# A transformer layer with a mixture of experts: the last two expert tiles without VectorE, plain second gathers, and the final normalising shared between two engines

## The reference, cut to what matters

```python
logits = x_flat @ w_router
top_vals, top_idx = jax.lax.top_k(logits, 2)
probs = jax.nn.softmax(top_vals, axis=-1)
h = jnp.einsum('nc,ecd->ned', x_flat, w_fc)        # 8 experts, 512 x 512
h = jnp.square(jax.nn.relu(h))
y = jnp.einsum('ned,edc->nec', h, w_proj)
out = jnp.einsum('nec,ne->nc', y, w_tok)           # weights of the two chosen experts
x = _layernorm(x + out, axis=-1)
```

## Time and profile before

| | |
|---|---|
| Median of 3 runs | 1472.44 us |
| The profiled execution | 1470.72 us |
| Its span, first to last instruction | 1469.0 us |
| TensorE busy | 1428.9 us (97%) |
| VectorE busy | 771.4 us (53%) |
| ScalarE busy | 727.3 us (50%) |
| GpSimd busy | 415.4 us (28%) |
| Granted TensorE clock, mean | 0.995 of full speed |

### The profile page before, as it was taken

One profiled execution on the slowest core, in us unless ns is written; L12 is line 12 of the kernel. 1 busy time (PEld: TensorE's weight loads), 2 busy tenths in 40 slices (PEclk: granted clock), 3 DMA queues, 4 the chain that ended last, 5 costly groups with the idle time before them and its releaser, 6 DMA issues. The chain is left out here.

```text
span 1469.0 us, 26596 instructions
## 1 busy us (share of the span) xinstructions
PE 1428.9 (97%) x7998; PEld 1209.6 (82%) x7999; DVE 771.4 (53%) x1813; ACT 727.3 (50%) x1633; POOL 415.4 (28%) x410
## 2 busy tenths in 40 slices
PE   8999999999999999999999999989999989999994
PEld 6888888888888888888888888878888867888883
DVE  6555655655555655555555565545555563333334
ACT  5665655655656565556565565622222223333334
POOL 1212121212112212122121121103333445345575
PEclk9999999999999999999999999999999999999997
DMA  5243323232323333233323235433348446665699
GB/s 176 77 129 93 107 93 127 86 114 85 115 93 107 111 111 100 100 98 102 108 93 128 93 107 179 144 123 125 136 121 224 123 172 215 253 247 200 211 199 235
DMA packets 86547, 200.45 MB, mean 136 GB/s; under 512 B 15856, under 2 KB 16496, under 8 KB 83184
## 3 DMA queue, kind: packets, MB, share of 16 engines
q1 hardware_dynamic: 75728, 149.66, 31.2%
q0 software_dynamic: 10784, 50.36, 12.0%
HBM read 160.05 MB, written 92.62 MB: 172 GB/s over the span
## 5 line engine op out<-in xcount | busy, mean ns | idle before, releaser
L378 POOL TENSOR_TENSOR small<-small,half 128x4 f32<-128x4 f32 x193 | 194.9, 1010 | 768.8 <-DVE small L408 768.8
L511 DVE CUSTOM_DVE_ANT_0 logit<-score_ps,bias 128x128 f32<-128x128 f32 (+3 forms) x256 | 124.8, 487 | 157.0 <-PE score_ps L650 117.6
L312 ACT ACTIVATE prob<-logit,small 128x128 f32<-128x128 f32 (+3 forms) x256 | 144.2, 563 | 120.5 <-DVE small L511 116.8
L663 PEld LDWEIGHTS y_ps<-vs,prob_t 128*128 128x128 f32 x1280 | 175.0, 191 | 20.4 <-issue 3.7
L663 PE MATMUL y_ps<-vs,prob_t 128*128 (+1 forms) x1280 | 184.7, 275 | 0.3 <-DVE x_now L412 0.3
L319 ACT ACTIVATE prob_t<-prob_ps 128x128 f32<-128x128 f32 (+3 forms) x256 | 111.6, 436 | 54.4 <-PE prob_ps L656 53.4
L894 ACT ACTIVATE yt_hi<-turn_ps,subln 128x512 fp32r<-128x512 f32 x60 | 41.0, 688 | 154.1 <-PE turn_ps L1188 150.2
L656 PE MATMUL prob_ps<-ident,prob 128*128 128x128 f32 x640 | 112.7, 274 | 3.2 <-ACT prob L312 3.0
L576 PE MATMUL v_ps<-w_hi,x_hi 128*128 (+1 forms) x256 | 106.8, 417 | 1.3 <-DVE w_lo L447 1.3
L576 PE MATMUL v_ps<-w_hi,x_lo 128*128 (+1 forms) x256 | 106.3, 415 | 0.0
L576 PE MATMUL k_ps<-w_hi,x_hi 128*128 (+1 forms) x256 | 103.2, 403 | 0.6 <-DVE w_lo L447 0.6
(11 more groups left out here) (250 smaller groups left out, 3421.5 us busy)
## 6 DMA issues: line engine op xcount, KB each, us to landing
slots_x<-in_zeros SPq DMA_DIRECT2D x64, 512.0 KB, 5.2
y_scratch<-x_now SPq DMA_DIRECT2D x65, 256.0 KB, 2.9
x_raw<-in_x_t SPq DMA_DIRECT2D x64, 256.0 KB, 2.8
slots_y<-in_zeros SPq DMA_DIRECT2D x64, 256.0 KB, 5.1
y_raw<-y_scratch SPq DMA_DIRECT2D x14, 1024.0 KB
w_raw<-in_w_experts POOLq DMA_DIRECT2D x7, 2048.0 KB
w_hi<-in_w_experts POOLq DMA_DIRECT2D x7, 2048.0 KB
w_raw<-in_w_all SPq DMA_DIRECT2D x16, 768.0 KB, 6.5
```

The source lines that it names most:

```text
L312: nc.scalar.activation(prob[:, 0:width], logit[:, 0:width], ACT.Exp, scale=-1.0, bias=least[:, h:h + 1], accum_out=row_sum[:, (i % 2) * HG ...
L378: nc.gpsimd.tensor_tensor(r, ms, half[:, :], ALU.pow).then_inc(ready, 1)
L511: nc.vector.tensor_tensor_reduce(out=logit[:, 0:width], in0=score_ps[:, 0:width], in1=bias[:, h, T - width:T], scale=1.0, scalar=3e38, op0 ...
L663: mm = nc.tensor.matmul(y_ps[:, h * D:(h + 1) * D], prob_t[:, j * P:(j + 1) * P], one(vs[:, bass.ds(now, 1), j, h * D:(h + 1) * D]), start ...
```

## The change

In slot steps 37 and 38 (`ALONE` and after) VectorE and SP have no part. ScalarE squares (from `relu`, with the Square function) and copies the low part; TensorE computes that low part: it multiplies the tile by the identity into the accumulator that already held the turned tile and then adds minus the identity times the high part (`turn_remainder`), between the sixth and seventh matmul of the next product, or at once in step 38. ScalarE issues the stores of the two slot tiles. (With 39 slot tiles, the branch for the rows of tile k + 2 is never taken in steps 37 and 38.)

The second gathers of tiles 8 to 15 go without addition to `w_raw`; VectorE adds them to `x1`. The aggregate of a tile stands right behind its statistics. Batches are 4, 4, 4 and 4 tiles. The root of the first batch is issued on GpSimd behind second gather 7, that of the second behind gather 11, the last two behind gather 15. VectorE normalises twelve tiles: 0 to 3 behind the statistics of tile 5, 4 to 7 behind those of 9, 8 and 9 behind those of 14, and 12 and 13 at the end; ScalarE normalises 10, 11, 14 and 15.

```diff
+        negative = sb("negative", [P, P], F32R)
-        END_BATCHES = ((0, 4), (4, 8), (8, 12), (12, 14), (14, 16))
+        END_BATCHES = ((0, 4), (4, 8), (8, 12), (12, 16))
+        PLAIN = range(8, 16)
+        ACT_TILES = (10, 11, 14, 15)
+        ALONE = SLOT_TILES - 2
...
@@ slots_sync @@
             def slot_step(k, b, h, y, q):
+                if alone(k):
+                    return
...
             for t in range(NT):
-                sp.wait_ge(fin_ready, t + 1)
+                done = sum(u in ACT_TILES for u in range(t + 1))
+                if t in ACT_TILES:
+                    sp.wait_ge(fin_scaled, done)
+                else:
+                    sp.wait_ge(fin_ready, t + 1 - done)
                 sp.dma_start(out_tiles[t], x1[:, t, :]).then_inc(fin_stored, 16)
...
@@ slots_gpsimd @@
-                gather(t, 1, second_gathered[t % GB])
-            pool.wait_ge(end_set_up, 1)
-            for first, last in END_BATCHES:
-                end_inverse_std(first, last)
+                if t in PLAIN:
+                    pool.indirect_dma_start(w_raw[:, t % GB, :], None, slots_y,
+                                            bass.IndirectOffsetOnAxis(ap=slot_y[:, 1, t:t + 1], axis=0))\
+                        .then_inc(second_gathered[t % GB], 16)
+                else:
+                    gather(t, 1, second_gathered[t % GB])
+                if t == GB - 1:
+                    pool.wait_ge(end_set_up, 1)
+                    end_inverse_std(*END_BATCHES[0])
+                if t == GB + RB - 1:
+                    end_inverse_std(*END_BATCHES[1])
+            end_inverse_std(*END_BATCHES[2])
+            end_inverse_std(*END_BATCHES[3])
...
@@ slots_scalar @@
+            nc.scalar.activation(negative[:, :], ident[:, :], ACT.Copy, scale=-1.0).then_inc(negative_set, 1)
...
             def slot_step(k, b, h, y, q):
                 round_hid(b, k)
+                if alone(k):
+                    act.wait_ge(hid_rest, k - ALONE + 1)
+                    nc.scalar.activation(ht_lo[:, b, :], ht_ps[b][:, :], ACT.Copy).then_inc(ht_ready, 1)
                 if more(k, 1):
                     rectify(1 - b, k + 1)
+                    if alone(k):
+                        act.wait_ge(relu_done, k + 2)
+                        nc.scalar.activation(hid[:, 1 - b, :], relu[:, :], ACT.Square).then_inc(hid_ready, 1)
...
                 scale_out(k, b, y, q)
+                if alone(k):
+                    act.wait_ge(yo_ready, k + 1)
+                    act.nop(nofuse=True)
+                    nc.scalar.dma_start(y_slot[k], yo[:, y, :]).then_inc(yo_stored[y], 16)
...
-            for t in range(NT):
-                act.wait_ge(mean_ready, t + 1)
+            for n, t in enumerate(ACT_TILES):
+                act.wait_ge(mean_ready, n // 2 + 1)
                 nc.scalar.activation(x1[:, t, :], x1[:, t, :], ACT.Identity, scale=end_rstd[:, t:t + 1],
-                                     bias=minus_mean[:, t:t + 1]).then_inc(fin_ready, 1)
+                                     bias=minus_mean[:, t:t + 1]).then_inc(fin_scaled, 1)
...
@@ slots_vector @@
             def slot_step(k, b, h, y, q):
+                if alone(k):
+                    return
...
+            def normalise_rows(first, last):
                 dve.wait_ge(end_rstd_ready, last)
-                nc.vector.scalar_tensor_tensor(minus_mean[:, first:last], end_mean_var[:, first:last, 0], -1.0,
-                                               end_rstd[:, first:last], ALU.mult, ALU.mult)\
-                    .then_inc(mean_ready, last - first)
+                if first >= GB:
+                    nc.vector.scalar_tensor_tensor(minus_mean[:, first + 2:last], end_mean_var[:, first + 2:last, 0], -1.0,
+                                                   end_rstd[:, first + 2:last], ALU.mult, ALU.mult).then_inc(mean_ready, 1)
+                    last = first + 2
+                for t in range(first, last):
+                    nc.vector.tensor_scalar(x1[:, t, :], x1[:, t, :], end_mean_var[:, t, 0:1], end_rstd[:, t:t + 1],
+                                            ALU.subtract, ALU.mult).then_inc(fin_ready, 1)
...
             for t in range(NT):
                 dve.wait_ge(second_gathered[t % GB], 16 * (t // GB + 1))
+                if t in PLAIN:
+                    if t == PLAIN[0]:
+                        dve.wait_ge(first_gathered[t // GB], 16 * GB)
+                    nc.vector.tensor_tensor(x1[:, t, :], x1[:, t, :], w_raw[:, t % GB, :], ALU.add)\
+                        .then_inc(rows_summed, 1)
+                    dve.wait_ge(rows_summed, t - PLAIN[0] + 1)
                 nc.vector.bn_stats(end_stats[:, t, :], x1[:, t, :]).then_inc(end_stats_done, 1)
-                if t >= 1:
-                    aggregate(t - 1)
+                aggregate(t)
+                if t % RB == RB - 1:
+                    bias_variance(t + 1 - RB, t + 1)
+                if t == RB + 1:
+                    normalise_rows(*END_BATCHES[0])
+                if t == GB + 1:
+                    normalise_rows(*END_BATCHES[1])
+                if t == NT - 2:
+                    normalise_rows(*END_BATCHES[2])
+            normalise_rows(*END_BATCHES[3])
...
@@ slots_tensor @@
+            def turn_remainder(out, src, hi, b, rounded, count, done):
+                pe.wait_ge(rounded, count)
+                for c in range(CT):
+                    nc.tensor.matmul(out[:, c * P:(c + 1) * P], src[:, b, c * P:(c + 1) * P], ident[:, :],
+                                     start=(c == 0), stop=False)
+                nc.tensor.matmul(out[:, :], negative[:, :], hi[:, b, :], start=False, stop=True).then_inc(done, 1)
```

More of the change, by code:

```diff
@@ L1312, in more, with alone @@
             return (k if isinstance(k, int) else YB * LOOPED - 1) + ahead < SLOT_TILES
+        def alone(k):
+            return isinstance(k, int) and k >= ALONE
         def slots_sync(sp):
@@ L1366, in slots_sync @@
             for t in range(NT):
-                sp.wait_ge(fin_ready, t + 1)
+                done = sum(u in ACT_TILES for u in range(t + 1))
[3 more added lines that the diff above has]
+                    sp.wait_ge(fin_ready, t + 1 - done)
                 sp.dma_start(out_tiles[t], x1[:, t, :]).then_inc(fin_stored, 16)
             sp.wait_ge(fin_stored, 16 * NT)
+            for y in range(YB):
+                sp.wait_ge(yo_stored[y], 16 * ((SLOT_TILES - 1 - y) // YB + 2))
         def slots_gpsimd(pool, token_step, inverse_std, dispatch, send_gates):
@@ L1619, in slots_vector @@
             for t in range(NT):
                 dve.wait_ge(second_gathered[t % GB], 16 * (t // GB + 1))
-                nc.vector.bn_stats(end_stats[:, t, :], x1[:, t, :]).then_inc(end_stats_done, 1)
-                if t >= 1:
-                    aggregate(t - 1)
[L1624 to L1629, removed]
@@ L1639, in turn_x, with times @@
                 mm.then_inc(xs_turned, 1)
-            def times(out, b, hi, lo, first_block, first=0, last=3 * CT):
+            def turn_remainder(out, src, hi, b, rounded, count, done):
[4 more added lines that the diff above has]
+                nc.tensor.matmul(out[:, :], negative[:, :], hi[:, b, :], start=False, stop=True).then_inc(done, 1)
+            def times(out, b, hi, lo, first_block, first=0, last=3 * CT, between=None):
                 for s in range(first, last):
                     c, part = divmod(s, 3)
+                    if s == 6 and between is not None:
+                        between()
                     a = (hi, hi, lo)[part][:, b, c * P:(c + 1) * P]
@@ L1652, in load_owner, with up @@
                 return pe.value_load(at, min_val=0, max_val=E - 1)
-            def up(b, e, count):
+            def up(b, e, count, between=None):
                 pe.wait_ge(xt_ready, count)
                 pe.wait_ge(we_split, WT * e + WT)
-                times(h_ps[b], b, xt_hi, xt_lo, expert_block(e)).then_inc(up_done, 1)
+                times(h_ps[b], b, xt_hi, xt_lo, expert_block(e), between=between).then_inc(up_done, 1)
             def turn_hid(b, k):
@@ L1663, in turn_hid, with down @@
                 mm.then_inc(hid_turned, 1)
-            def down(b, e, k):
+            def down(b, e, k, between=None):
                 pe.wait_ge(ht_ready, k + 1)
-                times(ye_ps[b], b, ht_hi, ht_lo, expert_block(e) + CT).then_inc(down_done, 1)
+                times(ye_ps[b], b, ht_hi, ht_lo, expert_block(e) + CT, between=between).then_inc(down_done, 1)
             last = (NT - 1) * NHG
@@ L1708, in slot_step, with hid_remainder, x_remainder @@
             def slot_step(k, b, h, y, q):
+                hid_remainder, x_remainder = None, None
+                if alone(k):
+                    if k == ALONE:
+                        pe.wait_ge(negative_set, 1)
+                    def hid_remainder():
+                        turn_remainder(ht_ps[b], hid, ht_hi, b, ht_rounded, k + 1, hid_rest)
+                    if more(k, 2):
```

(8 more changed lines are left out.)

10 lines of the change are left out of this document (5 added, 5 removed).

## The result

The changed kernel has a median of 1477.33 us (19 runs, 1473.51 to 1483.6), the kernel before 1472.08 (19 runs, 1468.48 to 1475.88). The ratio is 1.0037, with a 95% interval of 1.0027 to 1.0047: slower by 5.3 us, where plus 0.8 was forecast. It lies in the stated range, but beyond the 0.3% that I had called no change.

A forecast was written before the change was run, and what follows sets the result against it. Bound: GpSimd's second gathers, its first root, then ScalarE normalising sixteen tiles. VectorE's 24.6 us from 1438.6, 0.3 stall, 6.1 serial end and 0.2 for stores give span 1469.8 against 1469.0: plus 0.8, median 1473.2 us, range 1469.0 to 1478.5.

The forecast's parts named there:

- the stated range: Whole kernel: median from 1469.0 to 1478.5 us, the bounds of the terms widened for the spread of the runs.
- The swap: Tail: ScalarE's 12.2 us behind GpSimd's gathers gives way to VectorE's 24.6 us from an earlier start, ending within a microsecond.
- VectorE alone is late next: Tail after the change: VectorE alone is late, busy from 1438.6 to about 1463.5 us.
- Off the path: Slot steps 37 and 38: added work moves the last slot's output 4.2 us, to about 1456.1, covered by a 10 us tail.
- the term for the store's issue: Slot step 38 on ScalarE: issuing a slot tile's store costs some 0.35 us, off the path.
- The wait on GpSimd: Between second gathers 7 and 8: first root holds GpSimd 5.4 us; VectorE's stall at gather 8 taken as 0.3 us.
- the first rival: Tail: GpSimd's side ends later than VectorE's work, plain gathers at 1.54 us; plus 3.3, median 1475.7; chance 0.18.
- the prediction's own signs: Tail: wrong if VectorE idles over 2 us, plain gathers take 1.5, normalising pitch leaves 0.47 to 0.58, or slot outputs land after 1462.
- Store and end 2.84: End of the kernel: from ScalarE's last normalised tile, the last store and the end of the span take 2.84 us.
- The lock: Gathers 8 to 15: VectorE and GpSimd keep each other from SBUF; plus 6.4 us, median 1478.8; chance 0.10.
- The two slow cases: Tail: SBUF lock, median 1478.8, chance 0.10; VectorE not freed, all ends 9.2 us later, 1482, chance 0.03.
- The bounds of my terms: Whole kernel: cheapest and dearest terms give a span of 1467.6 to 1472.5 us, minus 1.4 to plus 3.5.

The follow-up runs named there:

- slots_kept: The changed kernel with slot steps 37 and 38 back on VectorE and SP as before; ratio to the kernel before 1.0088.
- alone_only: The kernel before with only the new last two slot steps, without VectorE and SP; ratio to the kernel before 1.0027.
- shared4: act_root with only the last four second gathers plain and ScalarE also normalising tiles 8 and 9; ratio to the kernel before 1.0004.
- no_hold: The changed kernel with the first two batches' roots both behind second gather 11, VectorE's normalising of tiles 0 to 7 later; ratio to the kernel before 1.0021.
- late_pool: The kernel before plus one GpSimd fill that waits until all sixteen tiles are normalised; ratio to the kernel before 1.0023.
- act_root: no_hold with the last batch's roots off GpSimd: square root on ScalarE, reciprocal on VectorE; ratio to the kernel before 0.9999.
- shared4_sp: shared4 with the store of slot tile 37 back on SP; ratio to the kernel before 0.9973, median 1466.99 us.

## Why the prediction was right or wrong

**The swap, right.** "VectorE alone is late next": the changed kernel's VectorE works from S to S + 26.6. Its busy part was forecast as 24.6 and measured as 24.3 (26.6 less 2.3 of idling): statistics 0.80 as taken, additions 0.69 and 0.03, normalisings 0.46 where I took 0.50. slots_kept confirms that the engine is serial: 9.2 us later at the start, 8.9 later at the end.

**Off the path, right in sum.** The last slot's output ended at S + 16.4 where 17.5 was forecast, and its cover held. But the term for the store's issue was thinner than it looked: 0.35 was taken, 0.39 came, and in alone_only and shared4 it was 1.5 and 1.9. And I had no term for a fall of TensorE's clock in the last slot step, which came in four of the seven experiments with the new slot steps (shared4 and alone_only among them). In those two that step decides.

**The wait on GpSimd, right in kind and short in size.** The hole is there and VectorE idles exactly at gathers 8 and 9. Taken 0.3 us, measured 2.3. Two terms were mis-sized: the root is followed by 0.89 us of waits and registers and not 0.30, and a plain gather lands after 4.8 to 5.4 us here, not 3.8. I had built 3.8 from a plain store; the adding gathers' own 5.9 to 6.3 was the nearer row. no_hold shows that this term costs 2.0 us. The idling is nearly what the first rival said (2 us and 0.5), but not for its reason: it had plain gathers at 1.54 us, and they took 0.95 to 1.03 but for the two beside VectorE's operations (1.42 and 1.46), and the last gathers were not waited for. By the prediction's own signs, more than 2 us of idling on VectorE meant wrong.

**"Store and end 2.84": the step that failed.** I took the distance between ScalarE's last tile and the end of the span as a store's. It was the later one of two ends: the store's landing, and GpSimd's drain 6.3 us behind its last root. Before, the drain cost only 0.3 us, which hid it. Before, ScalarE still had 3.7 us of queued tiles to do when the last root was done (from 1462.50, that is 1461.80 and 0.70 by its timeline, to 1466.16); after, it has only the two tiles of that root (1472.05 to 1473.80). So the drain comes later against ScalarE's end. Measured 4.8; late_pool and act_root show the mechanism from both sides, plus 3.9 us and minus 1.4 behind ScalarE's end. The stores were mis-sized beside it. 0.2 was added for four of them coming at once, but they take 0.9: 3.0 us from ScalarE's end to SP's branch, after and in act_root, against 2.1 before and in alone_only.

Together: 2.0 for the idling, 1.1 for the drain (1.4 less 0.3) and 0.7 for the stores (0.9 less 0.2) too little, 0.4 too much in the other terms: 0.8 becomes 4.2.

**The lock, wrong as a rival, visible as a cost.** GpSimd and VectorE seem to hinder one another: the plain gather at 1449.61, beside four normalisings, took 1.42 where the next took 0.97, the root of tiles 8 to 11 beside an addition 1.34 and not 1.01. These are tenths, a few times. The Trainium skill (SBUF — State Buffer, Who interferes with whom) speaks of an exclusive lock for the whole VectorE operation; a single operation of 0.46 us held for its length would give just such 0.45, so the rows don't speak against the rule, only against my price of a standstill through all four. Nor do they single out the normalisings: in no_hold a plain gather beside one addition (from 1449.47) took the same 1.42.

**The chances.** The two slow cases had 0.13, and neither is what happened. The bounds of my terms reached from minus 1.4 to plus 3.5; the measured plus 5.3 lies outside them. It lies in the stated range only because that was widened for the spread of the runs. So that the range held is luck: no case had the drain or the dearer stores in it.

## What to carry to other kernels

Read what closes the program before pricing the last stretch: each engine's closing drain, not only the last store. An engine with a long drain should do its last work early, or the work should be elsewhere; the same root on other engines was worth 2.2 us here, 1.4 of it behind ScalarE's end. And a root or any other wait put into a queue of DMA issues is paid twice, as the wait and as the landing of what stands behind it; and a store moved to a compute engine costs that engine an issue that took 0.4 us in some executions here and 1.5 or 1.9 in others, for a reason not found.

## What was unexpected of the hardware

- GpSimd's closing drain ended 6.3 us after its last instruction, be that a root of 1.0 or 0.7 us or a fill of 0.1 (changed, before, late_pool). In act_root, with GpSimd's last root at 1456.3 (S + 15.9), it was over long before the end of the span. All traces but two have the 6.3; in shared4 and shared4_sp, where the last root runs right behind the last gather, it was 7.7 and 8.3, and why isn't known.
- ScalarE's issue of one 256 KB store took from 0.34 to 1.87 us, and the DMA share beside it doesn't sort the short from the long (0.39 us at 0.92, 1.87 at 0.57).
- TensorE's granted clock fell in the last slot step of some executions and not of others, with the same slot code and the same 0.39 us of issue: 0.67 from 1454 to 1458 in act_root, full in no_hold.
- Plain gathers landed 3.6 to 7.0 us after their start (changed, no_hold), and 6.7 to 7.7 in shared4_sp, hardly sooner than adding ones (5.9 to 6.3) though the issue is 0.97 against 1.54. What they wait for wasn't tried.
